# A selective state-space block: the causal convolution reads the input projection from PSUM instead of from a copy

## The reference, cut to what matters

```
x = x + mamba(layernorm(x))          # x: (2, 2048, 256)
x = x + ffn(layernorm(x))            # 256 -> 1024 (butterfly folded in), gelu, 1024 -> 256

xz = x @ in_proj_w.T                 # (2, 2048, 1024)
x_inner, z = split(xz, 2)            # 512 channels each
xc = causal_conv(x_inner, 4 taps per channel, 3 zeros ahead) + conv_b
x_conv = silu(xc)
x_dbl = x_conv @ x_proj_w.T          # delta (1), B (16), C (16) per token
y  = selective scan over the 2048 steps (x_conv, softplus(delta), B, C)
y  = (y + x_conv * D) * silu(z)
out = y @ out_proj_w.T
```

## Time and profile before

| | |
|---|---|
| three runs | 651.51 us median (647.25 to 653.49) |
| profiled execution, first to last instruction | 646.1 us (no other time of this execution is given) |
| TensorE busy, mean granted clock | 562.6 us (87%), 0.941 |
| VectorE busy | 455.0 us (70%) |
| ScalarE busy | 298.5 us (46%) |
| GpSimd busy | 170.8 us (26%) |

### The profile page before, as it was taken

The page is one execution under the profiler, slowest core; times in us unless marked ns, Lnnn a source line. Parts: engine busy times, 40 slices in busy tenths (PEclk is TensorE's granted clock), DMA queues, the critical chain, the costliest instruction groups (busy, mean ns, idle before and its releaser), DMA issues.

```text
span 646.1 us, 8976 instructions
## 1 busy us (share of the span) xinstructions
PE 562.6 (87%) x2996; PEld 436.3 (68%) x2996; DVE 455.0 (70%) x867; ACT 298.5 (46%) x495; POOL 170.8 (26%) x140
## 2 busy tenths in 40 slices
PE   4496974867999998888999997979999997979996
PEld 3263733655789866466898864667899764847896
DVE  5376789987746579896656669796556789877432
ACT  3255565326324585517135684427045766053252
POOL 3245397524002005052003023051012042250010
PEclk9697887779999999998999997989999999979999
DMA  6631200010010000000010000000020000000000
GB/s 136 105 19 2 66 0 1 1 31 3 2 32 33 33 2 1 1 33 3 0 32 32 33 0 0 1 32 2 1 64 0 33 0 0 1 0 1 1 33 33
DMA packets 33077, 12.96 MB, mean 20 GB/s; under 512 B 22003, under 2 KB 32499, under 8 KB 33044
## 3 DMA queue, kind: packets, MB, share of 16 engines
q1 hardware_dynamic: 31988, 11.54, 7.9%
q10 hardware_dynamic: 1056, 1.05, 0.5%
HBM read 8.39 MB, written 4.19 MB: 19 GB/s over the span
## 4 chain that ended last, share of the span: by engine, by line
PE 52%; DVE 27%; issue 6%; ACT 6%; SPq 5%; POOL 2%; DVEq 0%; DMA 0%; ACTq 0%; POOLq 0%
PE acc L910 14%; PE wide L899 12%; DVE xc L1353 7%; PE wide L768 6%; PE wide L888 4%; PE wide L877 3%; PE wide L870 3%; SPq L415 3%; DVE x1b_xn L1291 2%; PE small L758 2%; PE wide L777 2%; POOL paths L544 2%; DVE mixed L1332 2%; DVE soft L1392 2%; DVE x1b_xn L1332 1%
## 5 line engine op out<-in xcount | busy, mean ns | idle before, releaser
L1070 ACT ACTIVATE hid_f<-wide,bias_up 128x512 f32<-128x512 f32 x64 | 44.0, 687 | 139.3 <-PE acc L910 127.4
L1353 DVE SCALAR_TENSOR_TENSOR xc<-xi,taps,xc 128x512 f32<-128x512 f32 x96 | 101.2, 1065 | 6.5 <-ACT xc L1099 4.2
L1370 DVE TENSOR_TENSOR hid_low<-hid_f,hid_high 128x512 fp32r<-128x512 f32 x64 | 44.3, 692 | 69.3 <-ACT hid_high L1171 68.7
L910 PE MATMUL acc<-w_down_high,hid_high 128*128 128x256 f32 x256 | 73.9, 289 | 1.6 <-DVE hid_low L1370 1.6
L910 PE MATMUL acc<-w_down_low,hid_high 128*128 128x256 f32 x256 | 71.8, 281 | 0.0
L910 PE MATMUL acc<-w_down_high,hid_low 128*128 128x256 f32 x256 | 71.7, 280 | 0.0
L888 PE MATMUL wide<-w_out,yg 128*128 128x256 f32 x256 | 58.5, 388 | 1.9 <-DVE yg L1503 1.9
L501 POOL TENSOR_TENSOR rstd<-var_eps,minus_half 128x4 f32<-128x4 f32 x16 | 19.0, 1185 | 152.7 <-DVE var_eps L1286 152.3
L569 POOL TENSOR_TENSOR c_place<-xd,row_in_block 128x1024 f32<-128x1024 f32 x8 | 15.5, 1938 | 153.1 <-DVE xd L1381 153.1
L888 PEld LDWEIGHTS wide<-w_out,yg 128*128 128x128 f32 x256 | 49.2, 194 | 9.2 <-issue 2.2
L768 PE MATMUL wide<-xnT_high,w_in_high 128*128 128x512 f32 x128 | 54.4, 425 | 0.2 <-DVE xnT_low L1364 0.2
(11 more groups left out here) (186 smaller groups left out, 1182.9 us busy)
## 6 DMA issues: line engine op xcount, KB each, us to landing
x_in<-in_L_attn_x_dram SPq DMA_DIRECT2D x8, 512.0 KB, 3.6
out_dram<-x1b_xn SPq DMA_DIRECT2D x8, 512.0 KB, 2.9
xc<-in_L_attn_in_proj_w_dram ACTq DMA_DIRECT2D x2, 512.0 KB, 7.1
xc<-in_L_ffn_W_exp_dram SPq DMA_DIRECT2D x1, 1024.0 KB, 5.1
low_w<-in_L_ffn_W_con_dram SPq DMA_DIRECT2D x1, 1024.0 KB, 6.0
raw_out<-n_L_attn_out_proj_w_dram SPq DMA_DIRECT2D x1, 512.0 KB, 6.0
low_w<-in_L_ffn_up_weights_dram SPq DMA_DIRECT2D x14, 4.0 KB
low_w<-_L_ffn_down_weights_dram SPq DMA_DIRECT2D x14, 4.0 KB
```

Of the source, the lines that this page charges most:

```text
L910: last = pe.matmul(acc[:, c, :], hid[h][:, j % HRING, c * P:(c + 1) * P], w_down[w][:, j, 0:DM], start=j == 0 and c % 2 == 0 and n == 0, s ...
L1070: ins = act.activation(out_ap, in_ap, how.pop("func"), **how)
L1353: ins = dve.scalar_tensor_tensor(xc[b][:, e, :], xi[:, e, tap:tap + TILE], taps[:, e, tap:tap + 1], xc[b][:, e, :], ALU.mult, ALU.add)
L1370: dve.tensor_tensor(hid[1][:, j % HRING, :], hid_f32[:, j % HRING, :], hid[0][:, j % HRING, :].bitcast(F32), ALU.subtract).then_inc(hid_re ...
```

## The change

The x blocks are no longer copied to `xi`. ScalarE writes the last tap with the bias into `xc` and saves the block's last three columns in `tail`. VectorE adds three carried columns (`carry`) to the head of the block, and then the three taps, reading the PSUM bank shifted by one to three columns. Its last tap releases the bank. Once for each b and tile, `carry_over` forms the columns for the next tile out of the tails. The x and z blocks alternate in the new `IN_ORDER`, which the bank order and TensorE's order follow. For b = 0 ScalarE applies silu to z as it reads the bank, so the separate silu over z is left for b = 1 only. ScalarE's order follows suit. VectorE's order of calls stays, with `carry_over` after the fourth convolution of each b. At the start, TensorE waits for all four parts of the input weights ahead of the first block.

```diff
+IN_ORDER = ((0, 4, 1, 5, 2, 6, 3, 7), (0, 4, 1, 5, 2, 3, 6, 7))
 WIDE_ORDER = (
-    [("in", e, 0) for e in range(8)] + [("xp", 0, 0)] + [("in", e, 1) for e in range(7)] + [("xp", 0, 1)]
+    [("in", e, 0) for e in IN_ORDER[0]] + [("xp", 0, 0)] + [("in", e, 1) for e in IN_ORDER[1][:7]] + [("xp", 0, 1)]
     + [("y", g, 0) for g in range(CB)] + [("out", 0, 0), ("out", 1, 0), ("in", 7, 1)]
     + [("up", j, 0) for j in range(4)] + [("y", g, 1) for g in range(CB)]
     + [("up", 4, 0), ("out", 0, 1), ("out", 1, 1)] + [("up", j, 0) for j in range(5, HB)]
...
@@ -171,8 +172,9 @@
         x_in = [sb(f"x_in{b}", [P, GR, DM]) for b in range(BATCH)]
         xn1 = [sb(f"xn1_{b}", [P, GR, DM]) for b in range(BATCH)]
         xnT = [sb(f"xnT_{part}", [P, MB, TILE], F32R) for part in PARTS]
-        xi = sb("xi", [P, CB, HALO + TILE])
-        halo = [sb(f"halo{b}", [P, CB, HALO]) for b in range(BATCH)]
+        tail = [sb(f"tail{b}", [P, CB, 2 * HALO]) for b in range(BATCH)]
...
@@ -934,32 +932,32 @@
                         down(k, b, j - HRING)
 
             def first_half(k, beside=lambda step: None):
-                for e in range(8):
+                for n, e in enumerate(IN_ORDER[0]):
                     in_projection(k, 0, e)
-                    if e % 2:
-                        beside(2 + e // 2)
+                    if n % 2:
+                        beside(2 + n // 2)
                 transposes(k, "ln1T", 1, xn1[1], norm1)
                 x_projection(k, 0)
                 tokens_first(k, 0)
                 xd_tokens_first(k, 0)
                 beside(6)
-                in_projection(k, 1, 0)
-                in_projection(k, 1, 1)
+                in_projection(k, 1, IN_ORDER[1][0])
+                in_projection(k, 1, IN_ORDER[1][1])
                 beside(7)
-                in_projection(k, 1, 2)
-                in_projection(k, 1, 3)
+                in_projection(k, 1, IN_ORDER[1][2])
+                in_projection(k, 1, IN_ORDER[1][3])
                 beside(8)
                 step_sums(k, 0)
                 beside(9)
-                in_projection(k, 1, 4)
+                in_projection(k, 1, IN_ORDER[1][4])
                 decayed_b(k, 0)
                 beside(10)
-                in_projection(k, 1, 5)
+                in_projection(k, 1, IN_ORDER[1][5])
                 decayed_c_start(k, 0)
                 spread_c(k, 0)
                 beside(11)
                 decayed_c_block(k, 0)
-                in_projection(k, 1, 6)
+                in_projection(k, 1, IN_ORDER[1][6])
                 off_diagonal(k, 0)
                 state_inputs(k, 0)
                 beside(12)
...
@@ -1078,33 +1077,26 @@
                 for m in range(MB):
                     take(k, name, m, b, xnT[0][:, m, :], tile_of(name, m, b)[:, :])
 
-            def place_halo(k, b):
-
-                act.wait_ge(convolved.handle, convolved.value(k, b, CB, ago=1))
-                act.wait_ge(halo_saved.handle, halo_saved.value(k, b, 1, ago=1))
-                act.activation(xi[:, :, 0:HALO], halo[b][:, :, :], ACT.Copy).then_inc(halo_moved.handle, 1)
-                act.wait_ge(halo_moved.handle, halo_moved.value(k, b, 1))
-
-            def save_halo(k, b):
-                act.wait_ge(xi_copied.handle, xi_copied.value(k, b, CB))
-                act.activation(halo[b][:, :, :], xi[:, :, TILE:TILE + HALO], ACT.Copy).then_inc(halo_saved.handle, 1)
-
             def first_tap(k, b, e):
 
                 bank = tile_of("in", e, b)
                 if e == 0:
                     act.wait_ge(gated.handle, gated.value(k, b, CB, ago=2))
                     written(act, k, "xtok", GR - 1, b, ago=2)
-                take(k, "in", e, b, xi[:, e, HALO:], bank[:, :], last=False).then_inc(xi_copied.handle, 1)
-                mark_read(act.activation(xc[b][:, e, :], bank[:, :], ACT.Identity, bias=tap_bias[:, e:e + 1],
-                                         scale=taps[:, e, TAPS - 1:TAPS]), "in", e, b)
+                    act.wait_ge(carried.handle, carried.value(k, b, 1, ago=2))
+                take(k, "in", e, b, xc[b][:, e, :], bank[:, :], last=False, func=ACT.Identity,
+                     bias=tap_bias[:, e:e + 1], scale=taps[:, e, TAPS - 1:TAPS])
+                act.activation(tail[b][:, e, 0:HALO], bank[:, TILE - HALO:TILE], ACT.Copy).then_inc(tapped.handle, 1)
 
             def copy_z(k, b, e):
                 take(k, "in", e, b, z[b][:, e - CB, :], tile_of("in", e, b)[:, :])
 
-            def silu_x(k, b):
-                for e in range(CB):
-                    act.wait_ge(convolved.handle, convolved.value(k, b, e + 1))
+            def gate_z(k, b, e):
+                take(k, "in", e, b, z[b][:, e - CB, :], tile_of("in", e, b)[:, :], func=ACT.Silu)
+
+            def silu_x(k, b, blocks=range(CB)):
+                for e in blocks:
+                    read(act, k, "in", e, b)
...
@@ -1171,20 +1163,19 @@
                 act.activation(hid[0][:, j % HRING, :], hid_f32[:, j % HRING, :], ACT.Copy).then_inc(hid_high.handle, 1)
 
             def first_half(k, beside=lambda step: None, scale=lambda n: None):
-                place_halo(k, 0)
                 first_tap(k, 0, 0)
+                gate_z(k, 0, 4)
+                beside(2)
                 first_tap(k, 0, 1)
-                beside(2)
+                gate_z(k, 0, 5)
+                beside(3)
                 first_tap(k, 0, 2)
+                gate_z(k, 0, 6)
+                beside(4)
+                silu_x(k, 0, (0, 1))
                 first_tap(k, 0, 3)
-                save_halo(k, 0)
-                beside(3)
-                copy_z(k, 0, 4)
-                copy_z(k, 0, 5)
-                beside(4)
-                silu_x(k, 0)
-                copy_z(k, 0, 6)
-                copy_z(k, 0, 7)
+                gate_z(k, 0, 7)
+                silu_x(k, 0, (2, 3))
                 beside(5)
                 high_parts(k, "ln1T", 1, ("in", 7, 0))
                 take_xd(k, 0)
@@ -1193,20 +1184,18 @@
                 load_exp_table()
                 beside(6)
                 exp_abs(k, 0)
-                place_halo(k, 1)
                 first_tap(k, 1, 0)
+                copy_z(k, 1, 4)
+                beside(7)
                 first_tap(k, 1, 1)
-                beside(7)
-                first_tap(k, 1, 2)
-                first_tap(k, 1, 3)
-                save_halo(k, 1)
+                copy_z(k, 1, 5)
                 beside(8)
                 exp_sums(k, 0)
                 beside(9)
-                copy_z(k, 1, 4)
+                first_tap(k, 1, 2)
                 exp_gaps(k, 0)
                 beside(10)
-                copy_z(k, 1, 5)
+                first_tap(k, 1, 3)
                 exp_diagonal(k, 0)
                 beside(11)
                 take_c_start(k, 0)
...
@@ -1346,16 +1334,26 @@
             start(dve, [vector_steps])
 
 
-            def convolve(k, b, e, chosen=range(TAPS - 2, -1, -1)):
-
-                read(dve, k, "in", e, b)
-                for tap in chosen:
-                    ins = dve.scalar_tensor_tensor(xc[b][:, e, :], xi[:, e, tap:tap + TILE], taps[:, e, tap:tap + 1],
-                                                   xc[b][:, e, :], ALU.mult, ALU.add)
+            def convolve(k, b, e):
+
+                bank = tile_of("in", e, b)
+                dve.wait_ge(tapped.handle, tapped.value(k, b, e + 1))
+                link(dve.tensor_tensor(xc[b][:, e, 0:HALO], xc[b][:, e, 0:HALO], carry[b][:, e, :], ALU.add))
+                for tap in range(TAPS - 2, -1, -1):
+                    back = TAPS - 1 - tap
+                    ins = dve.scalar_tensor_tensor(xc[b][:, e, back:TILE], bank[:, 0:TILE - back], taps[:, e, tap:tap + 1],
+                                                   xc[b][:, e, back:TILE], ALU.mult, ALU.add)
                     if tap:
                         link(ins)
                     else:
-                        ins.then_inc(convolved.handle, 1)
+                        mark_read(ins, "in", e, b)
+
+            def carry_over(k, b):
+
+                later = bass.AP(tail[b], 0, [[CB * 2 * HALO, P], [2 * HALO, CB], [1, HALO], [1, HALO]])
+                link(dve.tensor_tensor(tail_taps[:, :, :, :], later, taps[:, :, 0:HALO].unsqueeze(2)
+                                       .to_broadcast([P, CB, HALO, HALO]), ALU.mult))
+                dve.tensor_reduce(carry[b][:, :, :], tail_taps[:, :, :, :], AXIS_X, ALU.add).then_inc(carried.handle, 1)
 
             def low_parts(k, name, b):
...
                 if g == 0:
                     written(dve, k, "out", 1, b, ago=1)
-                    dve.wait_ge(z_ready.handle, z_ready.value(k, b, 1))
+                    if b == 0:
+                        read(dve, k, "in", 2 * CB - 1, b)
+                    else:
+                        dve.wait_ge(z_ready.handle, z_ready.value(k, 0, 1))
...
@@ -1547,6 +1548,7 @@
                 at[:] = [k, 0]
                 for e in range(CB):
```

(39 more changed lines are left out.)

8 lines of the change are left out of this document (3 added, 5 removed).

## The result

The changed kernel takes 673.47 us (median of 4 runs, 669.8 to 677.18) against 650.21 for the kernel before (4 runs, 647.25 to 653.49): ratio 1.0352, 95% interval 1.0291 to 1.0413. The forecast was 666, in a range of 653 to 676.

The account below looks back on a forecast made before the run. Bound by waits between TensorE and VectorE in a tile's first half. Three steady tiles of 1.8 + 2.4 give 12.6, the first 2.5: 15 us on 646.1, 661; median 5.4 higher, so 666, range 653 to 676 (own 658 to 673).

Parts of the forecast that it names:

- rival 3: VectorE's PSUM taps are held up by GpSimd as well; three tiles cost 9 us more, 675; chance 0.10.
- the low bound: Whole kernel: 7 us for the steady tiles with the first tile at 2, given as 656.
- the walk through B: Steady tile's second stage step by step: late bank release idles TensorE nearly 5 us, sums at 392.9 instead of 386.5.
- Stage A, +1.8: Input projection of b = 0: two TensorE stalls of 0.9 at z5 and z7; 1.8 us longer, bounds 1.4 and 2.6.
- Stage B, +2.4: Input projection of b = 1 with scan preparation for b = 0: about 2.4 us longer, bounds 0.9 and 3.8.
- The term of 7.2: The 2.4 us added to the input projection of b = 1, taken over three steady tiles.
- First tile, +2.5: z5 and weight products wait for the first taps, held-up taps shrink: 2.5 us longer, between -7.2 and 4.2.
- The adds, 0.20 each: Eight three-column VectorE adds per tile, 0.20 us each; GpSimd may hold one up to about 1 us.
- The PSUM tap, 0.77, free of GpSimd: VectorE tap reading PSUM takes 0.77 us with link, 2.3 for three, and is not held up by GpSimd.
- ScalarE's work, nothing: Taking 32 copies of 0.60 us and four silus of z off ScalarE gains nothing.
- After B both orders are alike.: Rest of the tile after the projection of b = 1: no difference, and no slack to give back.
- Rivals 1 and 2: 1: relief reaches the path, 631 or 641, chance 0.12; 2: stall cheaper, within 1%, 657, chance 0.14.

Follow-up runs that it names:

- xproj_copy_b0: Changed kernel with ScalarE copying the x blocks of b = 0 to SBUF again, b = 1 still read in PSUM: 664.7 us, ratio 1.024.
- early_taps: Changed kernel with VectorE's first-tile taps of x0 and x1 put ahead of its wait for the small loads: 665.7 us, ratio 1.024.
- old_order_no_adds: copy_both_old_order without the three-column adds and carry_over, so that part of the computation is left out: 650.0 us, ratio 1.000.
- pad: Changed kernel with 64 more already met waits on VectorE ahead of its loop, no work changed: 672.5 us, ratio 1.033.
- warm: Changed kernel with eight more TensorE products in the idle ahead of z5 of b = 1, results overwritten: 669.5 us, ratio 1.029.
- copy_both_old_order: Changed kernel with both projections copied to SBUF again and blocks in the old order, x0 to x3, then z: 662.1 us, ratio 1.016.
- before_early: Kernel before the change, with its first two convolutions put ahead of VectorE's wait for the small loads: 643.8 us, ratio 0.988.

## Why the prediction was right, point by point

**Sign and size.** Slower was given 0.75, and it was slower by 3.6%. The forecast made 15 us; the medians say 23. The mechanism named, the late release of the bank, is shown; it has half of the loss, 10.9 us. That 673.5 lies in the range of 653 to 676 is in part luck: it lies just above the forecast's own 658 to 673, and near its top bound of 674, which was made of dearer steady tiles and not of the first tile, the adds and the loop edge that filled it. The 675 of rival 3 comes nearer than 666, by a mechanism that didn't occur. Two steps of the working don't add up either: the low bound, 651.5 + 7 + 2, is 660.5 and not 656, and the walk through B has the sums at 392.9 where 388.4 + 2.6 + 1.5 makes 392.5. Neither moves the forecast of 666 by more than about 1 us.

**Stage A, +1.8.** Measured 1.9 in each tile, with the two stalls at z5 and z7. Their rows show 0.68 and 0.67 of idle; by the starts of the matmuls around them (383.07 to 384.49 for two steps of 0.23) each costs about 0.95, for the 0.9 forecast. xproj_copy_b0 takes it away.

**Stage B, +2.4.** In the tile walked it was 40.43 against 38.15, +2.28. Softplus to x_projection(1) was forecast at 405.3 - 380.5 = 24.8 and is 24.8; to the ready m_mat 28.9, and is 28.6. Inside, errors cancel: the idle was 3.88 and not nearly 5, because x0's add wasn't held up (0.16), and z5 ran half at full clock, so the sums came 1.0 us sooner than in the walk (11.4 after softplus, not 12.4). But the clock stayed low for longer, and x2 with the decayed products (411.4 to 416.0) took 4.6 where the walk had 3.2. What failed is the step from this tile to the others. In the kernel before, line 847 took 3.62 in this tile and 1.88 in the two others, where the clock had not fallen, with the same wait of 3.00. The second and the third tile, TensorE before:

```profile
254.34 0.63 PE L825 MATMUL small<-ident,c_start 128*128 128x128 f32 x4 [3.00 <-DVE c_start L1436]
254.81 1.88 PE L847 MATMUL small<-c_place,in_block 128*128 128x512 f32 x4
...
394.60 3.62 PE L847 MATMUL small<-c_place,in_block 128*128 128x512 f32 x4
```

So the two others were 1.4 us shorter and lost 2.83 and 3.68. The term of 7.2 was 8.8.

**First tile, +2.5.** This is the term that was mis-sized most: 11.5 in the traces (less by an unknown part in the medians, which leave 23.3 - 5.7 - 8.8 - 3.4 = 5.4 if the other stages are taken from the traces, and the scatter is 6 to 8). "z5 now waits for the first of them" was right, but it was costed like a steady tile, where VectorE is a microsecond late. Here it stood in a DMA wait until 35.88, which the prediction named (36.98) without asking what TensorE does until then: 8.38 us of idle at the lower clock. With taps ahead of the wait (early_taps) that idle is gone. What the wait has in the cost of the change stays open: by the medians the change costs 21.9 us with it out of the way and 23.3 as it stands. So does how the 11.5 divide between this wait and the adds: with the banks freed by ScalarE the first tile was 8.8 and 10.3 longer (two traces), with taps ahead of the wait there were 2.0 left, and the two don't add up.

**The adds, 0.20 each.** Right for most (median 0.16), wrong where they meet GpSimd: "up to about 1 us in the first block of B" fits the longest (0.999), but carry_over's 0.45 was some 2 us twice in the first tile (its product 1.79 and 1.91; behind the first VectorE still waited 0.23 us for ScalarE, so that one cost nothing there). In the kernel with copied input in the old order, taking them out removes the whole excess, 1.6 points of the ratio, or 10.7 us. About 3.1 of this is the loop edge, which goes by where the code lies. So much for the copied kernels, where the taps are held up as well; what the adds cost beside taps from PSUM no run takes by itself.

**The PSUM tap, 0.77, free of GpSimd.** Right: 746 to 751 ns over all 96, beside GpSimd or not, where the copied taps went up to 2.5 us. Rival 3 is out. The Trainium skill's rule (SBUF — State Buffer, Who interferes with whom) agrees with this, and so it does for the adds, which have two SBUF inputs. The Trainium skill's larger fixed cost for a PSUM source (VectorE: DVE Perf Modes, the table under the errata) doesn't show: the median was 752 ns with the copy and is 748.

**ScalarE's work, nothing.** Right for the silus of z: old_order_no_adds keeps the new silu and equals the kernel before. It copies the x blocks again, though, so that the 32 copies taken away are worth nothing isn't tested.

**"After B both orders are alike."** True of the work (88.08 against 88.09 in the last tile), wrong at the loop edge: 3.4 us that the forecast put at nothing and that no work of the program accounts for (pad).

**Rivals 1 and 2** stay out: the first needed x0's bank by the time TensorE wants it, and TensorE waited 3.88 us for it; in the second the clock doesn't fall, but it fell, and warm shows that this is worth 1.5 to 2.3 us per tile.

## What to carry to other kernels

When the reader of a buffer changes from one engine to another, cost the release by the time at which the new engine *gets to* it, in each place where the code runs: a prologue in which that engine waits for a load is not a steady tile. A tiny instruction that contends cost here what its neighbour had left to run (0.15 or 1.92 us for three columns), so count contending instructions, not elements. Where two kernels each scatter by 6 to 8 us, one trace of each places a loss in a stage, but its size has to be checked against the medians. And before a tile is taken as the reference, look whether the others show the same clock.

## What the runs showed of the hardware

- VectorE at its loop's back edge executed nothing for 2.9 and another 2.2 us with no semaphore in the way. With 24 or 64 instructions more ahead of the loop the whole idle is 2.0 and 2.7 us instead of 5.0, and ends with TensorE's product. That it is the supply of instructions is my reading; shown is that moving the code, with the same work, takes it away.
- The same idle of 3.00 us ahead of the same matmuls let the clock fall in one of three tiles of the kernel before (line 847: 1.88, 3.62, 1.88). Behind the 3.41 of copy_both_old_order the same products took 1.88, 2.82 and 3.50. Stage B of one tile was 1.4 us longer for it (38.15 against 36.7).
- GpSimd is held up as well: its six path products took 14.41 us beside taps from SBUF, 12.29 in before_early with no taps beside them, and 12.30 in the changed kernel.
